# Cell and attention kernel: the last amplitude in the Sigmoid's scale, biases written by TensorE transposes, new instruction orders

## The chip, the cores and the metric

The kernel runs on one NeuronCore of a Trainium2 chip, as one launch. It is programmed engine by engine: TensorE (PE) multiplies and transposes, VectorE (DVE) and ScalarE (ACT) work elementwise, GpSimd (POOL) does small pieces and issues some DMAs, SyncE (SP) issues most DMAs. Each engine runs its own list of instructions in order, and semaphores are the only ties between the lists. The metric is the device time in microseconds, the median of several runs.

## The reference

A batch of 32 sequences of 64 tokens, 256 features, all f32. A sequence-dependent linear map feeds an attention with 16 heads of 16 features, in which five sines of each score are weighted and summed before a sigmoid. The result is normalised and added to x. Then comes an adapter chosen by language (down to 64, relu, up to 256, layer norm with its own gamma and beta), and a recurrence over the 32 sequences as time steps, with 64 tokens as its batch:

```python
for fi, freq in enumerate(FREQS):                     # 5 frequencies
    scores = scores + alpha[h, fi] * sin(TWO_PI * sim / freq + phi[h, fi])
w = sigmoid(scores); w = w / (sum(w, -1) + 1e-10)
out = layernorm(w @ v @ Wo.T + bo) * gamma + beta     # x = x + out
h = relu(hidden @ W1[lang] + b1[lang]);  x2 = hidden + h @ W2[lang] + b2[lang]
def step(c, xt):                                      # 32 steps
    ft = sigmoid(xt @ wf.T + c @ uf.T + bf); it = sigmoid(xt @ wi.T + c @ ui.T + bi)
    gt = tanh(xt @ wc.T + c @ uc.T + bc)
    return ft * c + it * gt, None
h = tanh(x @ wo.T + c_final @ uo.T + bo)              # x = x + h
```

## The kernel before

The 32 sequences form five groups of 4, 8, 8, 8 and 4 (`SIZES`). Per group: condition (one weight per sequence), turn to feature rows, queries, keys, values. The queries are spread into a block form by DMAs from SP (`spread_q(g, c)`; the first group is masked on the engines instead). Scores of a group are cut into as many *units* of 128x512 as it has sequences: for groups of eight a unit is one pair of heads (`pairs_of`), for the two groups of four it is two pairs, and everything with an amplitude or a phase is then two pieces of 256 columns.

For each unit `angle(n, f)` makes an integer phase for frequency f, either on ScalarE or on VectorE: ScalarE has the last `ON_ACT[n]` of the five frequencies, VectorE the others (105 of 160 on ScalarE). `wrap(n)` on VectorE masks all five at once, `sines(n)` on ScalarE takes the sines of all five, `add_sine(n, f)` on VectorE multiplies by the amplitude and adds up (f = 0 multiplies only), and `weights(n)` on ScalarE takes the sigmoid. `weighted(n)` on TensorE multiplies with the values, `divided` on VectorE divides by the sum.

The rest goes in eight parts of four sequences (q = 0 to 7): `turned`, an output row (`output_bias`: ScalarE writes the centred bias bo into PSUM, 128x512), `output_projection`, which adds on top of it, `squares`, `residual`, `turn_residual`, `adapter_down`, `hidden(q, 0)` (add b1), `hidden(q, 1)` (maximum with 0), `adapter_up`, `adapted`, `moments`, `normalise`, `turn_normed`, `modulated`, `shifted_language`. GpSimd computes the roots and issues three accumulating DMAs a part.

Cell step n needs a bias in its PSUM bank (`pg[n % 2]`, 128x384), written by ScalarE right after the tanh of step n-2, then `input_gates(n, 0 and 1)`, `state_gates(n)`, the tanh `gates(n)` on ScalarE, `cell_step(n, 0 and 1)` on VectorE, `state_turned(n)` on TensorE and `state_copy(n)` on VectorE. Sigmoids of the gates are taken as tanh of half the argument, so weights and biases are halved once (`halved`, `first_biases`). The output parts (`output_part`) are kept by ScalarE until the last state is known; the tail adds, takes a tanh and adds the residual.

The order on every engine is written out by hand, call by call, over all stages: neighbouring groups, parts and cell steps are interleaved. Products of the identity with itself, without use for the result, stand between the first stages on TensorE: 11 ahead of the first condition and 78 behind it. A product in f32 is two pieces in the trace, a transpose one. Four slots hold the angles of units in work (`SLOTS`). `LATE = 32` and `SUMMED = ()` switch two other variants off.

## Time and profile before

| what | us |
|---|---|
| median of 3 runs | 340.19 (338.52 to 341.05) |
| span of the profiled execution, first to last instruction | 337.2 |
| TensorE busy | 289.4 (86%) |
| VectorE busy | 285.0 (85%) |
| ScalarE busy | 270.5 (80%) |
| GpSimd busy | 49.4 (15%) |
| mean granted TensorE clock | 0.967 |

For the profiled execution only its span is known, and the durations all come from it. The rows of the last section but one are read so: PE is TensorE, PEld its weight loads, DVE VectorE, ACT ScalarE, SPq SyncE's own queue; L1667 is a line of the kernel; `sc<-ang,small,sc` is output and inputs by the program's names; `x19` is the number of pieces. Pieces on TensorE are pipelined: their durations overlap, and what one costs is better read from the distance of starts. A timeline merges neighbours of one kind, and a piece on VectorE or ScalarE can begin a little ahead of the end of its predecessor.

### The profile page before, as it was taken

How to read it: one execution, taken by the hardware profiler on the slowest of the kernel's cores; microseconds unless marked ns; L12 is line 12 of the kernel's file. 1: busy time of each engine (PE TensorE's matmuls, PEld its weight loads, DVE VectorE, ACT ScalarE, POOL GpSimd, SP SyncE). 2: the span in 40 equal slices, each digit the busy share in tenths (PEclk: the TensorE clock that was granted, in tenths of full speed). 3: DMA queues.
4: the chain of work that ended last, by engine and by line, in shares of the span. 5: the costliest groups of instructions: out<-in, count | busy, mean ns of one | idle time of the engine just before them, and what ended most of it. 6: DMA issues, size and time to landing. Idle time of an engine off the chain costs nothing.

```text
span 337.2 us, 7386 instructions
## 1 busy us (share of the span) xinstructions
PE 289.4 (86%) x2670; PEld 179.2 (53%) x2670; DVE 285.0 (85%) x617; ACT 270.5 (80%) x405; POOL 49.4 (15%) x58
## 2 busy tenths in 40 slices
PE   5979698396898899898999998899987998999873
PEld 5767278364455755454565544455653554433342
DVE  3189989969999999999999998999998999445256
ACT  1299999979999999999999999999999874323123
POOL 5000110012020004141000215302013212210000
PEclk9999999876999999999999999999997999999978
DMA  5688057563052485017723022700324150210006
GB/s 169 215 253 331 13 112 194 117 188 72 0 90 57 85 263 109 0 27 168 186 31 106 25 34 52 146 8 15 90 72 64 29 130 2 34 31 2 0 18 230
DMA packets 32230, 31.76 MB, mean 94 GB/s; under 512 B 10690, under 2 KB 24130, under 8 KB 32194
## 3 DMA queue, kind: packets, MB, share of 16 engines
q1 hardware_dynamic: 27266, 26.46, 28.7%
q0 software_dynamic: 4352, 4.20, 8.0%
q10 hardware_dynamic: 576, 0.64, 0.7%
q8 instruction: 21, 0.34, 0.4%
q14 instruction: 15, 0.12, 0.1%
HBM read 23.15 MB, written 2.10 MB: 75 GB/s over the span
## 4 chain that ended last, share of the span: by engine, by line
DVE 40%; ACT 21%; PE 17%; issue 10%; SPq 6%; DMA 2%; POOL 2%; DVEq 0%; ACTq 0%
DVE sc L1667 12%; ACT ang L1150 6%; DVE ang L1652 5%; PE pg L696 4%; ACT ang L1159 3%; DVE ang L1643 3%; SPq L343 3%; DVE fc L1806 2%; DVE sc L1665 2%; ACT gat L1205 2%; PE pf L606 2%; DVE vz L1633 1%; PE pr L670 1%; PE pf L526 1%; ACT sc L1141 1%
## 5 line engine op out<-in xcount | busy, mean ns | idle before, releaser
L1667 DVE SCALAR_TENSOR_TENSOR sc<-ang,small,sc 128x512 f32<-128x512 f32 (+1 forms) x160 | 97.8, 637 | 1.5
L1159 ACT ACTIVATE ang<-ang,qs 128x2560 f32<-128x2560 int32 x32 | 77.4, 2426 | 0.4 <-DVE ang L1652 0.2
L1150 ACT ACTIVATE ang<-sc,phase 128x512 int32<-128x512 f32 (+1 forms) x126 | 72.3, 641 | 0.7 <-DVE sc L1667 0.7
L687 PE MATMUL pg<-gate_w,zT 128*64 128x384 f32 x256 | 51.8, 504 | 1.1 <-ACT pg L1201 0.5
L696 PE MATMUL pg<-gate_u,cT 128*64 128x384 f32 x256 | 47.8, 494 | 3.0 <-DVE cT L1815 2.9
L1652 DVE TENSOR_SCALAR ang<-ang 128x2560 int32<-128x2560 int32 x32 | 47.4, 1483 | 1.9 <-ACT ang L1150 1.8
L1205 ACT ACTIVATE gat<-pg 128x384 f32<-128x384 f32 x32 | 15.6, 486 | 28.2 <-PE pg L696 28.1
L1643 DVE TENSOR_SCALAR ang<-sc,phase 128x256 int32<-128x256 f32 (+1 forms) x74 | 27.1, 406 | 4.7 <-ACT sc L1141 4.7
L696 PEld LDWEIGHTS pg<-gate_u,cT 128*64 128x64 f32 x256 | 16.6, 136 | 23.5 <-issue 14.8
L687 PEld LDWEIGHTS pg<-gate_w,zT 128*64 128x64 f32 x256 | 15.4, 137 | 18.6 <-issue 12.8
L1806 DVE SCALAR_TENSOR_TENSOR fc<-gat 128x256 f32<-128x256 f32 x32 | 13.4, 419 | 12.4 <-ACT gat L1205 12.2
L606 PE MATMUL pf<-qm,kT 64*64 64x128 f32 x512 | 18.8, 284 | 5.4 <-DMA qm<-qT 3.1
L624 PEld LDWEIGHTS pav<-vz,sc 128*64 128x64 f32 x512 | 18.1, 137 | 9.9 <-issue 5.6
L624 PE MATMUL pav<-vz,sc 128*64 128x34 f32 x512 | 19.7, 224 | 3.8 <-DVE atq L1687 2.9
L1141 ACT ACTIVATE sc<-pf 128x512 f32<-128x512 f32 x32 | 17.5, 592 | 4.1 <-PE pf L606 4.0
L1170 ACT ACTIVATE sc<-sc 128x512 f32<-128x512 f32 x32 | 19.2, 623 | 1.8 <-DVE sc L1667 1.7
L606 PEld LDWEIGHTS pf<-qm,kT 64*64 64x64 f32 x512 | 14.8, 138 | 10.4 <-issue 8.5
L526 PE MATMUL pf<-yT,wq 128*128 128x512 f32 (+1 forms) x40 | 16.1, 524 | 4.8 <-DVE yT L1619 3.4
L441 POOL TENSOR_SCALAR rs<-var 128x2 f32<-128x2 f32 x8 | 4.3, 536 | 104.3 <-ACT x L1186 104.3
L648 PE MATMUL pr<-wo,stage 128*128 128x256 f32 x64 | 17.8, 419 | 1.9 <-ACT pr L1179 1.8
L732 PE MATMUL pr<-wout,zT 128*128 128x256 f32 x64 | 17.9, 420 | 0.7 <-DVE zT L1796 0.7
L1665 DVE TENSOR_SCALAR sc<-ang,small 128x512 f32<-128x512 f32 (+1 forms) x40 | 16.4, 426 | 0.3 <-ACT ang L1159 0.2
(137 smaller groups left out, 482.9 us busy)
## 6 DMA issues: line engine op xcount, KB each, us to landing
wc<-in_cond SPq DMA_DIRECT2D x30, 257.0 KB, 3.4
w<-in_up SPq DMA_DIRECT2D x32, 128.2 KB, 2.6
wa<-in_down SPq DMA_DIRECT2D x32, 66.0 KB, 2.2
xt<-in_xt SPq DMA_DIRECT2D x8, 256.0 KB, 2.9
xt<-rows POOLq DMA_DIRECT2D x8, 256.0 KB, 4.2
w<-x POOLq DMA_DIRECT2D x8, 256.0 KB, 4.8
xg<-in_x SPq DMA_DIRECT2D x3, 512.0 KB, 5.7
qm<-qT SPq DMA_DIRECT2D x48, 32.0 KB, 2.2
```

What stands on the lines that cost most here:

```text
L606: mm = pe.matmul(pf[u * L:(u + 1) * L, r, k * P:(k + 1) * P], kT[r * L:(r + 1) * L, c, b * L:(b + 1) * L], qm[r * L:(r + 1) * L, b + (SPRE ...
L624: mm = pe.matmul(pav[r, col:col + 2 * HV], at[:, b * L:(b + 1) * L], vz[:, b, p, :, :].rearrange("p u d -> p (u d)"), start=True, stop=True)
L687: pe.matmul(pg[n % 2][u * L:(u + 1) * L, 0:GCOLS], zT[:, q % 2, kc, t * L:(t + 1) * L], gate_w[:, kc, u, :], start=False, stop=(kc == KC - ...
L696: mm = pe.matmul(pg[n % 2][u * L:(u + 1) * L, 0:GCOLS], cT[:, kc, :], gate_u[:, kc, u, :], start=False, stop=(kc == KC - 1), skip_group_ch ...
L1141: act.activation(sc[:, lo:lo + 2 * nb * L].rearrange("p (k b n) -> p b k n", k=2, n=L)[:, h * PB:(h + 1) * PB], pf[:, r, :].rearrange("p ( ...
L1150: op = act.activation(ang[:, n % SLOTS, f, r], unit(n)[:, r], ACT.Identity, scale=TURN / FREQS[f], bias=phase[:, p * NF + f:p * NF + f + 1])
L1159: act.activation(a.bitcast(F32), a, ACT.Sin, scale=2 * PI_LOW / TURN, bias=qs[:, 3:4]).then_inc(sine_ready, 1)
L1205: act.activation(gat[:, 0:GCOLS], pg[n % 2][:, 0:GCOLS], ACT.Tanh).then_inc(gate_ready, 1)
L1643: op = dve.tensor_scalar(ang[:, n % SLOTS, f, r], unit(n)[:, r], TURN / FREQS[f], phase[:, p * NF + f:p * NF + f + 1], ALU.mult, ALU.add)
L1652: dve.tensor_scalar(a, a, (1 << TURN_BITS) - 1, None, ALU.bitwise_and).then_inc(angle_ready, 1)
L1665: op = dve.tensor_scalar(unit(n)[:, r], sine, amp, None, ALU.mult)
L1667: op = dve.scalar_tensor_tensor(out=unit(n)[:, r], in0=sine, scalar=amp, in1=unit(n)[:, r], op0=ALU.mult, op1=ALU.add)
```

## The change

1. *Sum of the sines.* New constants `lead` (the amplitude of the last frequency, shifted by 2e-12 where it's below 1e-12) and `ratio` (amplitude over `lead`). `add_sine(n, 0)` adds the first sine, times its ratio, to the fifth sine; three further fused steps follow. The sigmoid gets `lead` as its scale, per partition and pair of heads, so that units of the first and last group need two activations.
2. *Gate bias.* For the steps in `BIAS_BY_PE` (14 of 32) three transposes of a broadcast bias put it into PSUM; ScalarE writes the other 18.
3. *Output row.* For parts 0 to 5 (`ROW_BY_PE`) four transposes put the row into PSUM. The row is turned once (`turn_output_row`) and kept by VectorE (`keep_output_row`). For parts 6 and 7 ScalarE writes it as before.
4. *Hidden layer.* Two instructions of 64 columns, each with add and maximum, in place of one add and one maximum of 128 columns.
5. *Shares.* `ON_ACT` sums to 93 instead of 105, so VectorE makes 12 more angles.
6. *Orders.* All engines' lists are rewritten. On SP the cell's constants are loaded ahead of the attention's, of x and of the weights of group 1, and the adapter loads of part 0 ahead of the first spread. The constants have one array more, the turned gate bias (128x384). On ScalarE the halving of biases and gate weights moves to the first group. On TensorE all 11 identity products ahead of the first condition go, and 63 instead of 78 remain behind it. On VectorE four additions of the tail come ahead of the first residual.

```diff
-ON_ACT = [2, 2, 3, 3, 3, 4, 3, 4, 3, 4, 3, 4, 3, 4, 3, 4, 3, 4, 3, 4, 3, 4, 3, 4, 3, 4, 3, 4, 3, 3, 3, 2]
+ON_ACT = [1, 2, 3, 1, 3, 4, 1, 4, 3, 4, 2, 4, 2, 3, 3, 4, 3, 4, 3, 3, 3, 3, 3, 3, 3, 4, 3, 4, 2, 3, 3, 2]
+LEAST = 1e-12
+BIAS_BY_PE = (0, 1, 2, 4, 6, 8, 10, 12, 14, 16, 17, 18, 24, 31)
+ROW_BY_PE = (0, 1, 2, 3, 4, 5)
...
@@ sync
+            load_rest_consts()
             load_attention_consts()
-
             load_x(1)
+            load_cond(1, 1)
+            load_cond(1, 3)
             load_cond(1, 0)
             load_cond(1, 2)
-            load_cond(1, 3)
-            load_cond(1, 1)
-            load_rest_consts()
-            spread_q(1, 0)
             load_rest(0, 0)
-            load_cond(2, 1)
             load_rest(0, 1)
             load_rest(0, 2)
+            load_rest(0, 3)
+            spread_q(1, 0)
+            load_cond(2, 2)
             load_x(2)
-            load_rest(0, 3)
+            load_cond(2, 1)
+            load_cond(2, 3)
             spread_q(1, 1)
...
@@ tensor
+            def turn_output_row():
+
+                pe.wait_ge(row_centred, 1)
+                for c in range(KC):
+                    mm = pe.matmul(pr[:, 1, c * P:(c + 1) * P], rows[:, 3, c * P:(c + 1) * P], eye[:, :],
+                                   start=(c == 0), stop=True, is_transpose=True, skip_group_check=True)
+                mm.then_inc(row_turned, 1)
+
+            def output_bias(q):
+
+                pe.wait_ge(at_ready, q + 1)
+                if q == 0:
+                    pe.wait_ge(row_kept, 1)
+                for j in range(2):
+                    for c in range(KC):
+                        pe.matmul(tiles(q)[:, j, c * P:(c + 1) * P], out_bT[:, c, :], eye[:, :],
+                                  start=(j == 0 and c == 0), stop=True, is_transpose=True, skip_group_check=True)
...
+            def gate_bias(n):
+
+                if n == 0:
+                    pe.wait_ge(bias_scaled, 1)
+                wait(pe, gate_ready, n - 1)
+                for c in range(GATES):
+                    pe.matmul(pg[n % 2][:, c * P:(c + 1) * P], gate_bT[:, c, :], eye[:, :],
+                              start=(c == 0), stop=True, is_transpose=True, skip_group_check=True)
...
             pe.wait_ge(eye_s, 16)
-            for k in range(2):
-                for c in range(GATES):
-                    pe.matmul(pg[k][:, c * P:(c + 1) * P], eye[:, :], eye[:, :], start=(c == 0), stop=True, skip_group_check=True)
-
             pe.wait_ge(eye_s, 16)
-            for _ in range(5):
-                pe.matmul(pct[:, :], eye[:, :], eye[:, :], start=True, stop=True)
             condition(0, 0)
...
@@ scalar
-                    act.activation(unit(n), unit(n), ACT.Sigmoid).then_inc(w_ready, 1)
+                if n == 0:
+                    act.wait_ge(amps_ready, 1)
+                act.wait_ge(score_ready, n + 1)
+                for p in pairs_of(n):
+                    r = pair_in(n, p)
+                    op = act.activation(unit(n)[:, r], unit(n)[:, r], ACT.Sigmoid, scale=lead[:, p:p + 1])
+                op.then_inc(w_ready, 1)
...
-                if n + 2 < B:
+                if n + 2 < B and n + 2 not in BIAS_BY_PE:
+                    act.wait_ge(bias_halved, 1)
                     act.wait_ge(gate_ready, n + 1)
-                    gate_bias(n + 2)
+                    act.activation(pg[n % 2][:, 0:GCOLS], gate_b[:, :], ACT.Copy).then_inc(bias_set, 1)
...
@@ vector
-                    amp = scal(C_ALPHA + p * NF + f)
-                    sine = ang[:, n % SLOTS, f, r].bitcast(F32)
-                    if f == 0:
-                        op = dve.tensor_scalar(unit(n)[:, r], sine, amp, None, ALU.mult)
-                    else:
-                        op = dve.scalar_tensor_tensor(out=unit(n)[:, r], in0=sine, scalar=amp, in1=unit(n)[:, r], op0=ALU.mult, op1=ALU.add)
-                op.then_inc(score_ready if f == NF - 1 else score_part, 1)
+                    other = ang[:, n % SLOTS, NF - 1, r].bitcast(F32) if f == 0 else unit(n)[:, r]
+                    op = dve.scalar_tensor_tensor(out=unit(n)[:, r], in0=ang[:, n % SLOTS, f, r].bitcast(F32),
+                                                  scalar=ratio[:, p * NF + f:p * NF + f + 1], in1=other, op0=ALU.mult, op1=ALU.add)
+                op.then_inc(score_ready if f == NF - 2 else score_part, 1)
...
+            def keep_output_row():
+
+                dve.wait_ge(row_turned, 1)
+                dve.tensor_copy(out_bT[:].rearrange("p c n -> p (c n)"), pr[:, 1, 0:KC * P]).then_inc(row_kept, 1)
...
+            def hidden(q):
+
+                dve.wait_ge(down_done, q + 1)
+                for j in range(2):
+                    op = dve.tensor_scalar(hT[:, q % 2, j, :], pr[:, q % 2, j * L:(j + 1) * L], w2[:, q % 2, j, D:D + 1], 0.0, ALU.add, ALU.max)
+                op.then_inc(h_ready, 1)
...
             tail_added(0)
             tail_added(1)
+            tail_added(2)
+            tail_added(3)
             tail_residual(0)
             tail_residual(1)
-            tail_added(2)
-            tail_added(3)
+            tail_added(4)
+            tail_added(5)
             tail_residual(2)
```

The orders of the last part on TensorE, before and after (steps 22 to 24, part 7):

```
before: state_gates(22) turned(7) turn_normed(6) state_turned(22) output_projection(7) input_gates(23, 1)
        state_gates(23) input_gates(24) input_gates(25, 0) state_turned(23) turn_residual(7) state_gates(24)
after:  state_gates(22) weighted(30) weighted(31) input_gates(23) state_turned(22) turned(7) state_gates(23)
        turn_normed(6) output_projection(7) state_turned(23) gate_bias(24) input_gates(24) state_gates(24)
```

## Rows read from the trace of the kernel before

**Rows 1.** stretches of the run; busy us and piece count per engine, granted TensorE clock, DMA share, GB/s
```profile
17.10:100.00 82.90, 66.62 (x622) 49.63 (x623) 74.40 (x144) 76.93 (x104) 8.15 (x8) 0.92 0.52 136
100.00:280.00 180.00, 163.60 (x1669) 96.05 (x1669) 175.46 (x380) 172.36 (x261) 31.56 (x33) 0.99 0.36 81
280.00:323.50 43.50, 38.06 (x251) 16.70 (x247) 21.98 (x64) 12.79 (x28) 5.29 (x8) 1.00 0.08 13
```

**Rows 2.** timeline of TensorE, 278 to 323 us: start, us, engine, line, operation
```profile
283.18 1.49 PE L696 MATMUL pg<-gate_u,cT 128*64 128x384 f32 x8
...
293.44 0.66 PE L534 MATMUL pr<-eye,x 128*128 128x128 f32 x4
294.02 1.51 PE L696 MATMUL pg<-gate_u,cT 128*64 128x384 f32 x8
...
309.17 1.51 PE L696 MATMUL pg<-gate_u,cT 128*64 128x384 f32 x8 [0.38 <-DVE cT L1815]
...
312.77 1.51 PE L696 MATMUL pg<-gate_u,cT 128*64 128x384 f32 x8 [0.38 <-DVE cT L1815]
```

**Rows 3.** VectorE by form, 100 to 280 us: group xcount, busy us, mean ns, idle before
```profile
L1643 DVE TENSOR_SCALAR ang<-sc,phase 128x512 int32<-128x512 f32 x24 | 11.0, 471 | 0.0
L1665 DVE TENSOR_SCALAR sc<-ang,small 128x512 f32<-128x512 f32 x19 | 9.1, 478 | 0.2 <-ACT ang L1159 0.2
```

**Rows 4.** VectorE by form, whole run
```profile
L1643 DVE TENSOR_SCALAR ang<-sc,phase 128x256 int32<-128x256 f32 x38 | 10.8, 344 | 2.5 <-ACT sc L1141 2.5
...
L1665 DVE TENSOR_SCALAR sc<-ang,small 128x256 f32<-128x256 f32 x16 | 4.9, 346 | 0.0
```

**Rows 5.** ScalarE by form, 100 to 280 us
```profile
L1150 ACT ACTIVATE ang<-sc,phase 128x512 int32<-128x512 f32 x56 | 36.8, 712 | 0.0
L1170 ACT ACTIVATE sc<-sc 128x512 f32<-128x512 f32 x26 | 15.4, 622 | 0.1
...
L1201 ACT ACTIVATE pg<-gate_b 128x384 f32<-128x384 f32 x22 | 10.9, 495 | 0.7
...
L1150 ACT ACTIVATE ang<-sc,phase 128x256 int32<-128x256 f32 x22 | 9.4, 496 | 0.0
...
L1179 ACT ACTIVATE pr<-rows 128x512 f32<-128x512 f32 x6 | 3.6, 595 | 0.2
```

**Rows 6.** ScalarE by form, whole run
```profile
L1112 ACT ACTIVATE qT<-pf,bqs,qs 128x512 f32<-128x512 f32 x6 | 4.6, 765 | 0.7 <-PE pf L526 0.7
...
L1119 ACT ACTIVATE kT<-pf,small 128x512 f32<-128x512 f32 x6 | 4.0, 672 | 0.0
...
L1231 ACT ACTIVATE gate_u<-gate_u 128x1024 f32<-128x1024 f32 x1 | 1.1, 1061 | 0.0
```

**Rows 7.** timeline of SP's DMA queue, 38 to 110 us
```profile
39.08 5.28 SPq L343 DMA_DIRECT2D qm<-qT  x8
...
55.99 6.34 SPq L343 DMA_DIRECT2D qm<-qT  x8
63.14 5.89 SPq L325 DMA_DIRECT2D wc<-in_cond  x6
```

**Rows 8.** timeline of TensorE, 56 to 100 us
```profile
64.08 1.10 PE L606 MATMUL pf<-qm,kT 64*64 64x128 f32 x32 [3.07 <-DMA qm<-qT]
```

**Rows 9.** timeline of VectorE, 36 to 72 us
```profile
59.10 2.45 DVE L1633 TENSOR_TENSOR vz<-pf,bv 64x1024 f32<-64x1024 f32 x2
```

**Rows 10.** timeline of TensorE, 0 to 18 us
```profile
2.78 2.93 PE L752 MATMUL pg<-eye 128*128 128x128 f32 x12 [2.78 <-DMA eye<-in_eye]
...
8.61 1.95 PE L548 MATMUL pf<-wc,xg 128*64 128x256 f32 x16 [0.91 <-DMA wc<-in_cond]
...
11.83 1.28 PE L763 MATMUL pct<-eye 128*128 128x128 f32 x10
```

**Rows 11.** timeline of VectorE, 322 to 337 us
```profile
326.64 1.29 DVE L1830 TENSOR_TENSOR go<-go,x 128x512 f32<-128x512 f32 x2
327.85 1.28 DVE L1824 TENSOR_TENSOR go<-go,hoc 128x512 f32<-128x512 f32 x2
329.23 1.29 DVE L1830 TENSOR_TENSOR go<-go,x 128x512 f32<-128x512 f32 x2
```

More of the change, by code:

```diff
@@ L273, in build @@
         banks = {4: pf[:, 0, :], 5: pf[:, 1, :], 6: pr[:, 0, :], 7: pr[:, 1, :]}
[L275 to L291 removed]
+        def slot_free(eng, n):
+            if n >= SLOTS:
+                eng.wait_ge(score_ready, n - SLOTS + 1)
         def shifted_wait(eng, q):
@@ L677, in turn_normed @@
                 turn(chunks(q), norm, 2, nt_done)
+            def gate_bias(n):
[5 more added lines that the diff above has]
+                              start=(c == 0), stop=True, is_transpose=True, skip_group_check=True)
             def input_gates(n, kc):
+                if kc == 0 and n not in BIAS_BY_PE:
+                    pe.wait_ge(bias_set, sum(k not in BIAS_BY_PE for k in range(n + 1)))
                 q, t = n // PB, n % PB
@@ L783, in _ @@
             condition(2, 1)
-            for _ in range(5):
-                pe.matmul(pct[:, :], eye[:, :], eye[:, :], start=True, stop=True)
+            warm(3)
             turn_tokens(1)
+            warm(5)
             queries(1, 0)
@@ L790, in _ @@
             keys(1, 1)
-            for _ in range(9):
-                pe.matmul(pct[:, :], eye[:, :], eye[:, :], start=True, stop=True)
+            warm(7)
             scores(2)
-            for _ in range(4):
-                pe.matmul(pct[:, :], eye[:, :], eye[:, :], start=True, stop=True)
-            scores(3)
             weighted(0)
             weighted(1)
-            for _ in range(5):
-                pe.matmul(pct[:, :], eye[:, :], eye[:, :], start=True, stop=True)
+            scores(3)
             weighted(2)
+            turn_output_row()
+            weighted(3)
+            warm(6)
+            turned(0)
             values(1, 0)
@@ L935, in _ @@
             state_turned(8)
-            input_gates(9, 1)
+            gate_bias(10)
+            input_gates(10, 0)
+            input_gates(10, 1)
+            scores(13)
             state_gates(9)
-            output_part(2, 1)
-            scores(13)
             turn_residual(3)
+            condition(7, 0)
+            turned(4)
+            adapter_down(3)
             state_turned(9)
-            turned(4)
-            input_gates(10, 0)
-            adapter_down(3)
-            input_gates(10, 1)
+            condition(7, 1)
@@ L954, in _ @@
+            keys(4, 0)
             turn_normed(3)
-            condition(7, 0)
-            condition(7, 1)
+            adapter_down(4)
+            queries(4, 1)
+            adapter_up(4)
+            input_gates(12, 0)
             state_turned(11)
-            input_gates(12, 0)
             input_gates(12, 1)
@@ L1318, in _ @@
             angle(9, 4)
+            tokens(3)
+            tokens(4)
+            sines(7, False)
             sines(8, False)
-            sines(9, False)
-            angle(10, 2)
             angle(10, 3)
             angle(10, 4)
+            queries(2, 0)
+            sines(9, False)
+            keys(2, 0)
+            queries(2, 1)
             angle(11, 1)
```

1124 lines of the change are left out of this document (515 added, 609 removed).

## The prediction

> **What bounds the kernel now.** I read the stretches first [rows 1]. From 17.1 to 100 us VectorE is busy 74.4 of 82.9 us and ScalarE 76.9; from 100 to 280 they are busy 175.5 and 172.4 of 180, and TensorE 163.6. From 280 to 323.5 TensorE alone is near full (38.1 of 43.5). So the long middle is held by two engines at once, with a third not far behind: an instruction taken from one of them is worth its own time only as far as the other two let it. Two other regimes stand around it. Before 100 us VectorE and ScalarE idle 8.5 and 6.0 us. After 280 us the cell recurrence sets the pace: two neighbouring state products start 3.60 us apart (309.17, 312.77) when nothing else is in the way, while the two steps from 283.18 to 294.02 took 10.84 us [rows 2]. Groups by form give the prices, in the middle and over the whole run [rows 3 to 6]; timelines give the rest.
>
> **The scores' sum (VectorE).** Per batch unit the first product, a plain multiplication, goes: the fifth sine is added unscaled in the first of four fused steps, and the common factor moves into the Sigmoid. In the middle 19 multiplications of 512 columns go, 9.1 us [rows 3]; units 28 to 31 have two of 256 columns each, and 4.9 us for the sixteen of eight units is 0.61 a unit, 2.4 us [rows 4]. Together 11.5 us. Before 100 us four units of the first group (2.4) and six of the second at 0.48 (2.9) give 5.3 us. That the first fused step now reads two sines instead of a sine and a score I take at nothing: same shape, same memory. With 10 ns more on each of the 40 first steps it'd be 0.4 us.
>
> **Angles moved from ScalarE to VectorE.** Twelve of 105: three in the first group, three in units 4 to 11, five in units 12 to 27, one in the last group. On VectorE one takes 0.471 us [rows 3], a pair of 256 columns 0.57 (10.8 us for 38 pieces [rows 4]); on ScalarE 0.712, or 0.85 a pair (9.4 us for 22 pieces [rows 5]). Middle: VectorE 5 x 0.471 + 0.57 = +3.0, ScalarE 5 x 0.712 + 0.85 = -4.4. Before 100 us: VectorE +3.1, ScalarE -4.7.
>
> **Sigmoid.** Its scale becomes a per-partition pointer. The nearest rows are two activations of 128x512 from PSUM, one with a pointer as bias (672 ns), one with pointers as scale and bias (765 ns): 93 ns for the pointer [rows 6]. For 24 units, 2.2 us. Units 0 to 3 and 28 to 31 need two pieces each instead of one: two angles of 256 columns take 0.85 us against 0.622 for the present Sigmoid [rows 5]; I take +0.3 a unit, between 0.2 and 0.4, so 1.2 before 100 us and 0.6 in the middle.
> The Trainium skill ("ScalarE: Activation LUTs", section "What ACT_TABLE_LOAD costs") says 93 ns for each such pointer, and the rows agree. By it this edit gives part of its gain back on the other full engine; the sum is the same by the page and by the rows.
>
> **Biases by TensorE.** In the middle ten of 22 gate biases leave ScalarE at 0.495 us, 5.0 us, and five of six output rows at 0.595, 3.0 us [rows 5]. The halving of the two gate matrices (1.06 us each [rows 6]) moves to before 100 us: 2.1. So ScalarE in the middle: 172.4 - 5.0 - 3.0 - 4.4 - 2.1 + 2.2 + 0.6 = 160.7. In their place TensorE gets 10 x 3 + 5 x 4 = 50 transposes of 128x128. Four such start within 0.58 us (293.44 to 294.02), 0.145 each, and last 0.66 with the pipe's end, 0.165 each [rows 2]: +7.3 to +8.3 us, from 163.6 to 171 or 172. The wait is not a new one: today the input product of step n waits for a bias that ScalarE writes after the tanh of step n-2, and the transposes wait for that same tanh. But the waiting instruction now stands in TensorE's own order, with scores, value products and state transposes queued behind it, and VectorE and ScalarE wait for those.
>
> **Hidden layer, kept row, constants.** The add and the maximum of the adapter become two pieces of half the columns, each with both operations, and one hand-over goes: -0.3 us in the middle, between -1 and 0. The copy of the turned output row is a piece of some 0.4 us before 100 us (an estimate from the 256-column pieces). The five new constants at the start lie in VectorE's wait for the first products.
>
> **The middle, summed.** VectorE 175.5 - 11.5 + 3.0 - 0.3 = 166.7, ScalarE 160.7, TensorE 171 to 172. VectorE with its present 4.5 us of idle time gives 171.2. TensorE's figure contains ends of the pipe that can overlap, so it's no hard floor, yet an engine this near to full will hold up the others. I take 173: a **gain of 7.0 us**. Bounds: 169 (half of VectorE's idle time gone as well, gain 11) and 180 (everything given back).
>
> **17 to 100 us.** VectorE -5.3 + 3.1 + 0.4 = -1.8; ScalarE -4.7 - 0.9 - 0.6 (two gate biases, one output row) + 0.4 (one more halving) + 2.1 + 1.2 = -2.5. I take **-1.8**. SP's order counts too. The spreads of the queries of group 1 start at 39.08 and 55.99, and the first lasts 5.28 [rows 7], so 11.6 us of other loads lie between. The nine adapter loads move ahead of the first spread, where SP stands idle; between the two there are now six condition weights and one of x. Six of the former take 5.89 us [rows 7]; with the x load some 6.5, so the second spread comes 5.1 us earlier. But the scores behind it start at 64.08 today [rows 8], and they also need the values, ready at 59.10 + 2.45 = 61.55 [rows 9]. That leaves **-2.0**, between 0 and -2.5. The constants' load moves ahead of x and the weights of group 1. I cost it at nothing, because VectorE has the first group's sines to add meanwhile, and at up to 4 us if those weights land late.
>
> **The start.** The products with the identity ahead of the first condition go. Twelve pieces of them took 2.93 us (0.24 each), ten equal ones later 1.28 (0.13) [rows 10]: TensorE began at the lower of its two levels (1.2 GHz) and rose after these pieces. Without them the first condition, 16 pieces in 1.95 us [rows 10], runs at the lower level: +1.9. The first turn and queries add some 0.4, the filler taken out between them gives 0.3 back. I take **+2.0**, between 0 and 4.
> The Trainium skill ("TensorE: Matmul & The Clock Gate", section "Part 4: PE-mode transpose") says that transposes don't count as busy for the clock in the way products do. No row here separates the two. By that rule the transposes wouldn't hold the clock up; that is rival 3.
>
> **The end.** The two slow steps cost 10.84 - 7.2 = 3.6 us more than two free ones, since the last part's output products stand between them. The new order puts those one step later, and three transposes (0.44) with them: **-1.0**, between 0 and -2. Behind the recurrence VectorE's additions and residuals go in pairs of 1.29 us; a pair of additions starts 1.21 after the residuals before it (326.64, 327.85), but residuals start 1.38 after additions (327.85, 329.23), which wait for a tanh [rows 11]. Four additions first save 0.17 twice: **-0.4**.
>
> **How the numbers follow.** -7.0 - 1.8 - 2.0 + 2.0 - 1.0 - 0.4 = -10.2 us. The profiled span is 337.2 us; the median of the runs, 340.2, lies 3.0 above it, and I keep that difference: span 327.0, time **330.0 us**.
>
> **Rivals.**
> (1) *TensorE becomes the bound of the middle.* Its 50 transposes stand in front of work that feeds the others, and the middle stays at 179. For it: the three engines need 167, 161 and 171 of 173 us, more than any stretch today. Against it: TensorE's figure counts pipe ends. Gain 1 instead of 7: 336.0 us; with the weights of group 1 late by up to 3 us, 339.
> (2) *All of the saving comes through.* ScalarE has 6 us more slack than VectorE, so idle time shrinks, and the start costs nothing: -11 - 1.8 - 2.5 - 2 - 0.5 = -17.8, 322.4 at the extreme, 325 as its middle. Against it: TensorE's load.
> (3) *The clock falls, and the time ends above today's.* From 17.1 to 100 us the granted clock is 0.92 on average [rows 1], that is 13 us at the lower level. Of the 78 filler products behind the start 63 remain, and 50 transposes stand in the middle. At the lower level TensorE, being full there, loses half a microsecond for each. It decides from 20 us of it in the middle (10.2 / 0.5); with 25 us, -10.2 + 12.5 = +2.3, 342.5 us. Against it: the middle has 0.99 today without a filler, so its own products hold the clock.
> (4) *The change doesn't do what it says*: ScalarE holds the middle, and a shorter sum on VectorE brings nothing. ScalarE would have to need 172; the rows give 161. Time 338 to 340.
>
> **Chances.** The forecast and its surroundings (326.5 to 334) 0.50, (2) 0.15, (1) 0.22, (3) 0.10, (4) 0.03. Some 1% is what a measurement of this kernel can tell from no change. Faster by over 1% (below 336.8): 0.50 + 0.15 + 0.13 of (1) = 0.78; within 1%: 0.12; slower: 0.10. The range 322 to 339 leaves out (3) and the far ends of (2), (1) and (4).
>
> **What the profile would show.** No plain multiplications of sines; 160 fused steps of today's length; Sigmoids of 512 columns near 715 ns; 18 gate biases and two output rows left on ScalarE; TensorE above 95% busy in its middle; the first condition at twice its length; the last unit's Sigmoid, and with it the end of the middle, some 8 to 9 us earlier. The prediction is wrong if VectorE's idle time in the middle grows by more than 6 us, if the clock there is below 0.9, or if group 1 starts more than 4 us later.

## The result, and the profile after

The changed kernel takes **322.5 us** (median of 4 runs, 320.6 to 324.2) against 339.4 of the kernel before beside it (338.5 to 341.1): a ratio of 0.949, 95% interval 0.944 to 0.954. The forecast was 330.0 with a range of 322 to 339. The sign was right and the time lies in the range, but at its lower edge: 16.9 us came where 10.2 were forecast. The profiled run took 323.4 us, 1.8 above its span. A run more than 1.5% above the fastest of its kernel is left out of median and ratio, which matters below for a_spold alone (five of ten).

The page of the changed kernel, first part and slices (each digit is the busy share of a fortieth of the span):

```profile
span 321.6 us, 7374 instructions
...
PE 285.4 (89%) x2686; PEld 177.5 (55%) x2686; DVE 274.6 (85%) x598; ACT 257.3 (80%) x378; POOL 51.6 (16%) x58
...
DVE  3049996999999999999999998999999998554265
ACT  1069998999999999999999999899999894422132
...
PEclk9999997998999999999999999999999999999997
```

VectorE's busy time fell from 285.0 to 274.6 us and ScalarE's from 270.5 to 257.3. The prediction's terms, added up, give VectorE 10.6 us less. So the work is as forecast, and the surprise is elsewhere: the span shrank by 15.6 us, more than either engine's work. To find the place, cut both runs at the same three events: the copy of the first scores (ScalarE), the last unit's Sigmoid and the last tanh of the gates. These are the stretches of the kernel before, with a cut at 100 us (columns as in [rows 1]):

```profile
17.11:100.00 82.89, 66.62 (x622) 49.63 (x623) 74.40 (x144) 76.93 (x104) 8.15 (x8) 0.92 0.52 136
100.00:282.01 182.01, 165.61 (x1693) 97.01 (x1691) 177.47 (x385) 173.11 (x262) 31.56 (x33) 0.99 0.36 80
282.01:321.53 39.52, 35.72 (x232) 15.60 (x228) 18.97 (x55) 11.55 (x26) 5.29 (x8) 1.00 0.09 15
```

and these the same of the changed kernel:

```profile
20.43:100.00 79.57, 69.54 (x646) 50.38 (x646) 75.59 (x146) 75.85 (x101) 10.63 (x8) 0.96 0.50 133
100.00:268.49 168.49, 163.18 (x1703) 99.02 (x1704) 166.01 (x361) 161.79 (x240) 32.53 (x34) 1.00 0.37 83
268.49:305.90 37.41, 35.51 (x245) 16.17 (x239) 18.71 (x54) 10.81 (x24) 4.05 (x7) 1.00 0.05 8
```

- Before the first scores: 17.11 to 20.43, **+3.3 us**.
- From the first scores to the last Sigmoid: 264.90 to 248.06, **-16.8 us**. VectorE's part of that: 251.9 busy becomes 241.6 (-10.3), and 13.0 idle becomes 6.5 (-6.6). The idle time shrank on both sides of the cut: 8.5 to 4.0 before 100 us, 4.5 to 2.5 behind it.
- The recurrence: 39.52 to 37.41, **-2.1 us**. These 2.1 aren't made in the recurrence itself, as the part on the recurrence below shows.
- From the last tanh to the end of the span: 15.7 in both.

The groups that the change touches, by form, whole run of the changed kernel (count | busy us, mean ns | idle just before them and its releaser), VectorE's first:

```profile
L1626 DVE SCALAR_TENSOR_TENSOR sc<-ang,ratio,sc 128x512 f32<-128x512 f32 x72 | 52.6, 743 | 0.2
L1615 DVE TENSOR_SCALAR ang<-ang 128x2560 int32<-128x2560 int32 x32 | 47.5, 1501 | 0.0
...
L1626 DVE SCALAR_TENSOR_TENSOR sc<-ang,ratio 128x512 f32<-128x512 f32 x24 | 17.8, 742 | 0.0
```

```profile
L1149 ACT ACTIVATE sc<-sc,lead 128x512 f32<-128x512 f32 x24 | 16.4, 714 | 0.3 <-DVE sc L1626 0.2
...
L1183 ACT ACTIVATE pg<-gate_b 128x384 f32<-128x384 f32 x18 | 8.9, 495 | 1.6
...
L1149 ACT ACTIVATE sc<-sc,lead 128x256 f32<-128x256 f32 x16 | 7.0, 500 | 2.0 <-DVE sc L1626 2.0
```

The plain multiplications of [rows 3, 4] are gone. A first step that reads two sines lasts 742 ns, one that reads a sine and a sum 743. The Sigmoid with its pointer lasts 714 ns (forecast near 715), and 18 gate biases and two output rows are left on ScalarE.

TensorE in the middle of the changed kernel, in stretches of 20 us:

```profile
120.00:140.00 20.00, 19.38 (x165) 11.18 (x162) 19.91 (x37) 19.97 (x28) 5.92 (x7) 1.00 0.44 114
140.00:160.00 20.00, 19.78 (x213) 10.90 (x211) 19.97 (x44) 19.47 (x27) 4.65 (x4) 1.00 0.51 104
160.00:180.00 20.00, 19.94 (x238) 13.00 (x235) 19.68 (x39) 19.75 (x27) 0.00 (x0) 1.00 0.45 109
```

All three engines read 97 to 100% here, and the granted clock is 1.00, its full level (2.4 GHz), with the transposes in and without a product of the identity. The case that the prediction thought unlikely, three full engines at once without one holding up another, is what the trace shows: VectorE idles 0.4 of these 60 us.

The clock before 100 us changed too: it reads 0.92 from 17 to 100 us before and 0.96 in the changed kernel, some 13 and 6 us at the lower level (1.2 GHz). A stretch where it is low in the kernel before:

```profile
67.00:76.00 9.00, 9.00 (x72) 6.15 (x72) 5.88 (x9) 6.60 (x12) 1.18 (x2) 0.71 0.65 190
```

TensorE is full there at a clock of 0.71, and VectorE idles 3.1 of its 8.5 us. In the changed kernel the same 9 us have a clock of 0.81, TensorE is busy for 6.6 us and VectorE for 8.9. So part of the idle time that vanished before 100 us may be the clock's. No run changes the clock alone, so its share isn't shown.

### The profile page after: what moved, and what is told of

Its sections match the earlier page's. It is cut to its first block, busy times and chain, and to the rows that moved or that the text cites. A ratio compares the mean times of both kernels' runs of the same rounds, so it can differ in the third digit from the quotient of the medians.

```text
span 321.6 us, 7374 instructions
## 1 busy us (share of the span) xinstructions
PE 285.4 (89%) x2686; PEld 177.5 (55%) x2686; DVE 274.6 (85%) x598; ACT 257.3 (80%) x378; POOL 51.6 (16%) x58
## 4 chain that ended last, share of the span: by engine, by line
DVE 39%; PE 32%; ACT 14%; issue 8%; DMA 3%; POOL 2%; SPq 1%; DVEq 0%; ACTq 0%; POOLq 0%
DVE sc L1626 12%; PE pg L694 7%; DVE ang L1615 5%; PE pg L685 5%; DVE ang L1606 5%; ACT ang L1130 4%; PE pf L491 3%; PE pav L589 3%; ACT ang L1139 3%; PE pf L571 2%; PE pf L547 2%; DVE fc L1761 2%; ACT sc L1121 2%; DMA w<-x 1%; DVE vz L1596 1%
## 5 line engine op out<-in xcount | busy, mean ns | idle before, releaser
L1626 DVE SCALAR_TENSOR_TENSOR sc<-ang,ratio,sc 128x512 f32<-128x512 f32 (+1 forms) x120 | 73.0, 637 | 0.4
L1130 ACT ACTIVATE ang<-sc,phase 128x512 int32<-128x512 f32 (+1 forms) x110 | 64.5, 650 | 0.0
L685 PE MATMUL pg<-gate_w,zT 128*64 128x384 f32 x256 | 50.8, 499 | 0.6 <-DVE zT L1751 0.4
L1606 DVE TENSOR_SCALAR ang<-sc,phase 128x256 int32<-128x256 f32 (+1 forms) x90 | 32.4, 412 | 2.6 <-ACT sc L1121 2.5
L1179 ACT ACTIVATE gat<-pg 128x384 f32<-128x384 f32 x32 | 15.6, 487 | 22.7 <-PE pg L694 22.3
L694 PEld LDWEIGHTS pg<-gate_u,cT 128*64 128x64 f32 x256 | 16.4, 136 | 22.1 <-issue 15.0
L513 PE MATMUL pf<-wc,xg 128*64 128x256 f32 x128 | 17.1, 416 | 9.5 <-DMA wc<-in_cond 8.8
L1149 ACT ACTIVATE sc<-sc,lead 128x512 f32<-128x512 f32 (+1 forms) x40 | 23.4, 628 | 2.3 <-DVE sc L1626 2.2
L1626 DVE SCALAR_TENSOR_TENSOR sc<-ang,ratio 128x512 f32<-128x512 f32 (+1 forms) x40 | 24.8, 637 | 0.0
L491 PE MATMUL pf<-yT,wq 128*128 128x512 f32 (+1 forms) x40 | 17.0, 550 | 1.9 <-DVE yT L1582 1.4
L729 PE MATMUL pct<-eye 128*128 128x128 f32 x126 | 18.2, 291 | 0.0
```

The costliest lines, as they stand in the source:

```text
L491: mm = pe.matmul(dst[:, 0:n], w[:, kc, oc * P:(oc + 1) * P], src[:, kc, 0:n], start=(kc == 0), stop=(kc == KC - 1))
L685: pe.matmul(pg[n % 2][u * L:(u + 1) * L, 0:GCOLS], zT[:, q % 2, kc, t * L:(t + 1) * L], gate_w[:, kc, u, :], start=False, stop=(kc == KC - ...
L694: mm = pe.matmul(pg[n % 2][u * L:(u + 1) * L, 0:GCOLS], cT[:, kc, :], gate_u[:, kc, u, :], start=False, stop=(kc == KC - 1), skip_group_ch ...
L1130: op = act.activation(ang[:, n % SLOTS, f, r], unit(n)[:, r], ACT.Identity, scale=TURN / FREQS[f], bias=phase[:, p * NF + f:p * NF + f + 1])
L1149: op = act.activation(unit(n)[:, r], unit(n)[:, r], ACT.Sigmoid, scale=lead[:, p:p + 1])
L1606: op = dve.tensor_scalar(ang[:, n % SLOTS, f, r], unit(n)[:, r], TURN / FREQS[f], phase[:, p * NF + f:p * NF + f + 1], ALU.mult, ALU.add)
```

## The experiments

The theory on record, **A**: the time follows the work taken off VectorE and ScalarE, and the new orders add a little. The rival, **B**: the orders carry the gain. Twelve kernels were run, in three groups of four, with the kernel before at 340.4 to 340.7 us in each, so times can be compared across them. The changed kernel itself ran beside one at 339.4; by its ratio it would be at 323.3 among them, so differences to its 322.5 are uncertain by about 1 us. Each kernel has one trace; what a stretch of it lasted is one execution's. "Operations" below are the folded amplitude, the transposed biases and rows, and the adapter's step; "shares" is the number of angles per unit that ScalarE makes; a "list" is an engine's order of work.

### The operations without the orders

b_sum is the kernel before with the folded amplitude alone. The core of the edit; the ratios and the Sigmoid's scale go with it:

```diff
-                    if f == 0:
-                        op = dve.tensor_scalar(unit(n)[:, r], sine, amp, None, ALU.mult)
...
+                    other = ang[:, n % SLOTS, NF - 1, r].bitcast(F32) if f == 0 else unit(n)[:, r]
```

> The kernel before, with the folded amplitude alone (four fused steps, Sigmoid with a pointer scale); its orders and shares stay. Theory A, two full engines share the middle: VectorE loses 16 us of pieces, ScalarE gets 5.6 us more and is full, so little comes through: 335 to 339 us. Rival, VectorE alone holds the middle: 10 us or more come through, 329 us or less.

Measured: 341.6 us, ratio 1.004 (1.001 to 1.007). VectorE has 11.3 us less to do (273.7), ScalarE 3.6 more (274.1), and the kernel is no faster: theory A's 335 to 339 is missed as well as the rival's 329. The middle, in stretches of 50 us:

```profile
100.00:150.00 50.00, 44.42 (x532) 28.74 (x531) 46.87 (x86) 49.78 (x72) 6.66 (x8) 1.00 0.41 96
150.00:200.00 50.00, 45.23 (x507) 26.82 (x507) 45.96 (x91) 49.72 (x73) 6.22 (x7) 1.00 0.44 96
```

ScalarE is full (99.5%), VectorE at 92 to 94%. With the old shares ScalarE is the fullest engine of the middle, and its Sigmoids have just become longer.

b_ops takes all of the new operations, with the old lists, shares and identity products (the new steps put at the places of the old):

```diff
+            gate_bias(0)
             input_gates(0, 0)
...
+            output_bias(1)
             output_projection(1, 0)
```

> All new operations (folded amplitude, 14 gate biases and 6 output rows by transposes, the merged hidden step), but the orders, the shares of the angles and the identity products of the kernel before. Theory A, the work taken from both full engines is the gain: 328 to 331 us, with VectorE's idle time before 100 us still near 8 us. Rival, the new orders and shares carry the gain: 334 us or more. Rival, TensorE is the bound with its 68 transposes: 336 us or more, with VectorE's idle time in the middle grown.

Measured: 340.2 us, ratio 0.998 (0.995 to 1.001). Now both are relieved (VectorE 285.0 to 274.4, ScalarE 270.5 to 265.3), and nothing comes of it:

```profile
100.00:150.00 50.00, 47.24 (x556) 30.72 (x556) 47.24 (x88) 49.03 (x72) 6.64 (x9) 1.00 0.39 93
150.00:200.00 50.00, 47.52 (x522) 28.31 (x520) 46.77 (x92) 48.75 (x69) 5.59 (x7) 1.00 0.44 95
200.00:250.00 50.00, 46.91 (x457) 28.91 (x455) 47.01 (x108) 45.44 (x64) 9.16 (x9) 1.00 0.31 65
```

No engine is full behind 200 us, and VectorE idles 3 us in each 50. What it waits for from 100 to 250 us (total us, times, longest) is spread over many hand-overs:

```profile
DVE fc L1776 <- ACT gat L1182: 2.1, 2, 1.4
DVE rden L1654 <- PE pav L590: 1.4, 3, 0.6
DVE sc L1641 <- ACT ang L1142: 1.2, 2, 0.8
...
DVE ang L1630 <- ACT ang L1133: 0.5, 1, 0.5
```

The last line is the wrap, which needs all five angles of its unit. In the whole run VectorE waits 3.7 us before its wraps, against 1.9 in the kernel before and 0.0 in the changed one, but only 0.5 of that falls between 100 and 250 us. Cut at the same events, b_ops is 2.7 us shorter from the first scores to the last Sigmoid (262.2, with VectorE's work 11.3 us less and its idle time 8.7 us more). It gives this back at the start (the copy of the first scores comes at 18.76, 1.7 later: its 11 products ahead of the condition all go to one bank, and the condition's 16 pieces take 3.68 us) and in the recurrence (1.6). So the operations do a little in the old lists, and the sum hides it.

Theory A, as I had put it, falls here: 328 to 331 was expected. The expectation's third case, TensorE as the bound with its 68 transposes, isn't excluded by b_ops alone: 336 us or more with VectorE's idle time grown is what came, TensorE is 94 to 95% busy, and ScalarE waits 2.4 us for its state products from 100 to 250 us. But b_sum, which has no transpose of a bias, is no faster either, so the transposes aren't needed to explain it. The transposes are also cheaper than forecast: TensorE is busy 5.8 us longer in b_ops than in b_sum, 0.085 for each of the 68 (0.12 by a_bias_act below), against the 0.145 to 0.165 of the prediction.

### The orders without the operations

a_old_ops_sh is the reverse: the changed kernel's five lists, with the old operations and the old shares. It still makes the new constants and keeps the turned row (VectorE is busy 287.5 us, 2.5 more than in the kernel before), and it has six products with the identity ahead of the first condition.

```diff
-ON_ACT = [1, 2, 3, 1, 3, 4, 1, 4, 3, 4, 2, ...]
+ON_ACT = [2, 2, 3, 3, 3, 4, 3, 4, 3, 4, 3, ...]
...
+            output_row(0)
...
             add_sine(0, 3)
+            add_sine(0, 4)
```

> The changed kernel's five order lists with every old operation put back (plain first product and five steps of a sum, one Sigmoid over the unit, all gate biases and output rows written by ScalarE, the adapter's bias and maximum in two steps) and the old shares of angles. If the orders alone carry the gain, the removed 10.4 us of VectorE and 13.2 us of ScalarE being slack: 322 to 326. If the new orders made VectorE the engine that limits, so that each microsecond of its work is one of the time: 322.5 + 10.4 and the start's 1.6 back, 331 to 334. If neither operations nor orders are worth anything without the other: 337 or more.

Measured: 347.1 us, ratio 1.019 (1.013 to 1.025), **slower than the kernel before**. B falls as well, in its simple form. The orders alone lose 6.5 us, the operations alone gain 0.2, and everything together gains 16.9.

### SyncE's and GpSimd's lists

a_loads is the changed kernel with the nine adapter loads of the first part back between the two spreads of group 1:

```diff
-            load_rest(0, 0)
...
-            load_rest(0, 3)
             spread_q(1, 0)
+            load_rest(0, 0)
...
+            load_rest(0, 3)
             load_cond(2, 2)
```

> The changed kernel with the nine adapter loads of part 0 put back behind the first spread of group 1, as in the kernel before. If these loads made the idle time between 60 and 100 us, the second spread comes some 10 us later, VectorE idles 4 to 6 us more before 100 us and the time is 326 to 328 us. Rival, the idle time vanished for other reasons: 322 to 323 us.

Measured: 327.1 us, ratio 0.962 (0.957 to 0.967), 4.6 above the changed kernel. The second spread in it, and then both spreads in the changed kernel (start, us, operation):

```profile
63.36 5.21 SPq L309 DMA_DIRECT2D qm<-qT  x8
```

```profile
41.76 6.25 SPq L309 DMA_DIRECT2D qm<-qT  x8
...
55.44 5.40 SPq L309 DMA_DIRECT2D qm<-qT  x8
```

The second spread starts 7.9 us later, the scores behind it 5.3 later (64.97 to 70.31), and in a_loads they have waited for it:

```profile
70.31 1.98 PE L571 MATMUL pf<-qm,kT 64*64 64x128 f32 x32 [6.57 <-DMA qm<-qT]
```

The changed kernel shows no such wait there. VectorE is busy 3.9 us less from 20 to 100 us (71.7 instead of 75.6).

a_spold puts both old lists of SyncE and GpSimd into the changed kernel, a_spnew adds the new ones to b_ops, b_sp to the kernel before.

```diff
-            load_rest_consts()
             load_attention_consts()
             load_x(1)
...
+            load_rest_consts()
+            spread_q(1, 0)
```

> The changed kernel with SyncE's and GpSimd's lists of before. Putting nine loads back behind the first spread alone cost 4.6. If that is all that SyncE's order is worth: 326 to 329. If the new compute orders stand on the new loads throughout: 333 or more. If the loads matter only there and elsewhere the old order is as good: 326.

Measured: 337.1 us (333.8 to 338.5; with the five left out 339.1, up to 343.4), ratio 0.986 (0.981 to 0.992): most of the gain is lost with two lists in which next to no computation stands. The waits of a_spold from 18 to 45 us (total us, times, longest):

```profile
ACT gate_bT L1199 <- DMA uout<-in_uout: 8.6, 1, 8.6
...
PE pf L500 <- ACT xg L1084: 8.2, 1, 8.2
DVE ang L1616 <- ACT ang L1131: 7.5, 1, 7.5
```

ScalarE's new list has the halving of biases and gate weights near its start, and it waits there for the last of the constants. With the constants loaded late, it stands 8.6 us with the copy of x and the angles of unit 2 queued behind it, and TensorE and VectorE stand with it. In the changed kernel the same stretch has no such wait. If that and the adapter loads (4.6) simply add up, they are 13.2 of the 14.6 us lost; the constants' place wasn't run by itself. The rest of SyncE's list is in it too: from 120 to 160 us VectorE idles 3.9 us in a_spold, and part of what it waits for hangs on condition weights that land late. Its clock from 20 to 100 us reads 0.91, the changed kernel's 0.96.

> All new operations, the old orders of TensorE, VectorE and ScalarE and the old shares, but the new lists of SyncE and GpSimd. If SyncE's order is worth its 4.6 us by itself: 335 to 337 (340.2 less 4). If it is worth something only where the compute lists ask for the earlier data: 339 to 342.

Measured: 336.4 us, ratio 0.987 (0.983 to 0.991): -3.8 to b_ops.

> The kernel before with the new lists of SyncE and GpSimd alone. With the new operations these lists gave 3.8 us in the old compute orders (340.2 to 336.4). If that gain is independent of the operations: 336 to 337. If it needed their saving: 339 to 342.

Measured: 338.3 us, ratio 0.996 (0.992 to 0.9995): -2.3. The number agrees with the 2.0 of the prediction (by the interval it may be 0.2 to 2.9), the way there only in part: the second spread starts at 53.22 instead of 55.99, 2.8 us earlier where 5.1 were forecast, and the scores behind it at 63.09, 1.0 earlier. The same loads are worth 2.3 us there, 3.8 with the new operations, and 14.6 (322.5 to 337.1) where the compute lists rely on them.

### One operation undone in the changed kernel

a_nofold has the old sum and Sigmoid in the new lists and shares (the plain product stands ahead of the first fused step).

```diff
             add_sine(0, 0)
+            add_sine(0, 1)
...
-                    op = act.activation(unit(n)[:, r], unit(n)[:, r], ACT.Sigmoid, scale=lead[:, p:p + 1])
+                act.activation(unit(n), unit(n), ACT.Sigmoid).then_inc(w_ready, 1)
```

> The changed kernel with the sum of sines as before (plain first product and four fused steps on VectorE, one Sigmoid over the unit on ScalarE); biases, rows, adapter, orders and shares stay new. VectorE has some 11 us more, ScalarE some 3.5 less. With everything undone and the old shares the time was 347.1, 24.6 above the changed kernel. If VectorE's work is what the new orders are built round: 333 to 338, over half of the 24.6. If the gate biases on ScalarE matter as much: 327 to 330.

Measured: 338.1 us, ratio 0.992 (0.989 to 0.994). VectorE is busy 291.4 us, 16.8 more than in the changed kernel (the expectation's 11 was the middle's part alone of the 16.8 in the prediction), and the time is 15.6 longer: 0.93 us for each us of VectorE. ScalarE's Sigmoids by form:

```profile
L1145 ACT ACTIVATE sc<-sc 128x512 f32<-128x512 f32 x32 | 19.5, 626 | 8.3 <-DVE sc L1625 8.3
```

ScalarE waits 8.3 us for VectorE's sums, 2.3 in the changed kernel. The fold that brought nothing in the old lists (b_sum) is worth nearly its full work in the new. One caution holds for this run and the next two: the new lists were made for the new operations and shares, so an operation put back costs its own time and also stands where no place was left for it. The two can't be told apart here.

a_bias_act gives all gate biases back to ScalarE, the first two right behind the halving, and has TensorE write six products with the identity into the gates' banks ahead of the first condition:

```diff
-BIAS_BY_PE = (0, 1, 2, 4, 6, 8, 10, 12, 14, 16, 17, 18, 24, 31)
+BIAS_BY_PE = ()
...
+            for k in range(2):
+                for c in range(GATES):
+                    pe.matmul(pg[k][:, c * P:(c + 1) * P], eye[:, :], eye[:, :], start=(c == 0), stop=True, skip_group_check=True)
```

> The changed kernel with all 32 gate biases written by ScalarE, none by transposes: 14 more ScalarE writes of about 0.49 us (6.9 us, most of them in the middle), 42 transposes less on TensorE (7.3 us in the profile). If ScalarE has no slack in the new orders: 327 to 331. If TensorE is the engine that limits, as its 97 to 99% between 120 and 200 us suggests: 318 to 321. If neither: 322 to 324.

Measured: 325.7 us, ratio 0.955 (0.952 to 0.957), +3.2. ScalarE has 5.8 us more (263.1), TensorE 2.1 less (42 transposes gone, 5.0 us or 0.12 each, and six products of together 2.9 us come). The time is what ScalarE's 5.8 us cost less what TensorE's relief gave, and only the sum is measured: 0.55 us for each us of ScalarE. So a bias costs more on ScalarE than on TensorE. That TensorE's 97 to 100% held up nobody isn't shown by it.

a_shares gives ScalarE back its twelve angles:

```diff
-ON_ACT = [1, 2, 3, 1, 3, 4, 1, 4, 3, 4, 2, 4, ...]
+ON_ACT = [2, 2, 3, 3, 3, 4, 3, 4, 3, 4, 3, 4, ...]
```

> The changed kernel with the old shares of angles: 12 angles of a frequency go from VectorE to ScalarE, at the place of ScalarE's other angles of the unit. VectorE's busy time falls by 5 to 8 us, ScalarE's rises by about 8 to 265. If VectorE's work alone sets the time: 315 to 319. If the two are balanced by the new shares, so that ScalarE's extra work shows: 325 to 330. If both have slack: 322 to 323.

Measured: 327.2 us, ratio 0.961 (0.955 to 0.966), +4.7, though VectorE has 3.6 us less to do; ScalarE has 6.7 more (264.0). So in the new lists an added us costs on either engine, as with two balanced engines, with the caution above.

### The start

a_warm puts 11 products with the identity ahead of the first condition, as many as the kernel before has there:

```diff
+            warm(11)
             condition(0, 0)
```

> The changed kernel with the 11 identity products put back ahead of the first condition. Theory: the first scores' copy comes 3.3 us earlier (17.1 instead of 20.4) and the whole follows: 319 to 320 us. Rival, the weights of group 1 or something else is late anyway and takes it back: 322 us, no difference.

Measured: 320.6 us (319.7 to 324.0), ratio 0.945 (0.938 to 0.952). This interval overlaps that of the changed kernel (0.944 to 0.954), so the 1.9 us aren't clear of the noise. a_best has 15, and 3 behind the condition:

```diff
+            warm(15)
             condition(0, 0)
             condition(0, 1)
+            warm(3)
             turn_tokens(0)
```

> The changed kernel with 15 identity products ahead of the first condition and 3 behind it (the first condition was still 3.46 us long behind 11, with 1.20 us idle ahead of it, against 1.95 us in the kernel before). If the idle time ahead of it is what halves the clock: condition 1.9 to 2.0 us, first scores' copy ends 3 us earlier than in the changed kernel, 318 to 319.5. If not: 320 to 322.5 as with 11.

Measured: 319.7 us (318.7 to 320.4), ratio 0.937 (0.935 to 0.940), **the lowest of all**, and clear of the changed kernel though not of a_warm. TensorE at the start of the changed kernel, of a_warm, of a_best, and of a_loads, which begins on TensorE as the changed kernel does:

```profile
8.84 3.68 PE L513 MATMUL pf<-wc,xg 128*64 128x256 f32 x16 [8.84 <-DMA wc<-in_cond]
13.30 1.11 PE L499 MATMUL pf<-eye,xg 128*128 128x128 f32 x4 [0.78 <-ACT xg L1083]
...
15.30 2.01 PE L491 MATMUL pf<-yT,wq 128*128 128x256 f32 x4
...
19.26 1.10 PE L571 MATMUL pf<-qm,kT 64*64 64x128 f32 x32 [0.42 <-ACT kT L1099]
```

```profile
2.63 5.03 PE L729 MATMUL pct<-eye 128*128 128x128 f32 x22 [2.63 <-DMA eye<-in_eye]
8.87 3.46 PE L513 MATMUL pf<-wc,xg 128*64 128x256 f32 x16 [1.20 <-DMA wc<-in_cond]
...
17.73 1.10 PE L571 MATMUL pf<-qm,kT 64*64 64x128 f32 x32 [0.42 <-ACT kT L1100]
```

```profile
2.66 6.33 PE L729 MATMUL pct<-eye 128*128 128x128 f32 x30 [2.66 <-DMA eye<-in_eye]
9.03 1.95 PE L513 MATMUL pf<-wc,xg 128*64 128x256 f32 x16
...
16.38 1.10 PE L571 MATMUL pf<-qm,kT 64*64 64x128 f32 x32 [0.42 <-ACT kT L1101]
```

```profile
9.01 3.61 PE L513 MATMUL pf<-wc,xg 128*64 128x256 f32 x16 [9.01 <-DMA wc<-in_cond]
13.40 0.66 PE L499 MATMUL pf<-eye,xg 128*128 128x128 f32 x4 [0.77 <-ACT xg L1083]
...
18.02 1.10 PE L571 MATMUL pf<-qm,kT 64*64 64x128 f32 x32 [0.42 <-ACT kT L1099]
```

The condition's 16 pieces last 3.68 us with nothing ahead of them, 3.46 with 11 products and then 1.20 us of idle time, and 1.95 with 15 products up to its start. The scores start at 19.26, 17.73 and 16.38, and the times go the same way: 322.5, 320.6, 319.7. But with nothing ahead of the condition the scores start anywhere from 17.69 (a_spold) over 18.02 (a_loads) and 18.10 (a_nofold) to 19.68 (a_shares), so a_warm's 17.73 isn't shown to come from its products. Only a_best's 16.38 lies apart. Which of its 15 and 3 products does it wasn't run separately.

### The table

| Operations | shares | SyncE, GpSimd lists | compute lists | us |
|---|---|---|---|---|
| old | old | old | old | 340.6 |
| new | old | old | old | 340.2 |
| old | old | new | old | 338.3 |
| new | old | new | old | 336.4 |
| new | new | old | new | 337.1 |
| old | old | new | new | 347.1 |
| new | old | new | new | 327.2 |
| new | new | new | new | 322.5 |

## Why the prediction was right, and where it was wrong

**Work.** Every count and duration came as forecast: VectorE -10.4 us (forecast -10.6), Sigmoids of 714 ns, the first step's two sines at no cost, the condition at nearly twice its length, TensorE above 95%.

**The middle.** This is the term that was mis-sized. The step that failed is: "an engine this near to full will hold up the others. I take 173". I had VectorE's idle time of the middle grow from 4.5 to 6.3 us; it fell to 2.5 behind 100 us. TensorE's 171 to 172 never came either: it is busy 163.2 us in the changed kernel's 168.5. The middle has 1703 of its pieces where the kernel before has 1693, not 50 more, since the new lists put other work of TensorE elsewhere, and a transpose added 0.085 to 0.12 us of busy time, not 0.145 to 0.165. From the first scores to the last Sigmoid the terms gave -10.8 (7.0, 1.8 and 2.0), and 16.8 came; of the missing 6.0, all is idle time of VectorE. a_bias_act shows that the transposes were the cheaper choice: with 42 of them turned back into writes of ScalarE the time rose.

**Why idle time fell.** The prediction weighed the operations for themselves and the compute lists at nothing. The runs show that neither counts alone: the operations in the old lists give 0.2 us, the lists without them cost 6.5. In the old lists and shares a relieved VectorE waits instead, for ScalarE and TensorE at many hand-overs, none of which stands out. In the new ones a us put back on VectorE costs 0.93 and the twelve moved angles 4.7. Before 100 us, where 4.5 of the 6.6 us of idle time went, the loads' order and the clock changed as well; a_loads gives the adapter loads 3.9 us of VectorE's time there. Rival (4), that a shorter sum brings nothing because ScalarE holds the middle, got 0.03; for the kernel before it comes near (b_sum), and what made it wrong for this change are the shares and orders. The time that came is that of rival (2), all of the saving (0.15): it names the shrinking idle time. Its start at no cost didn't come.

**SyncE's order.** Forecast -2.0; in the kernel before it is -2.3 (b_sp), in part by luck, since the scores there come 1.0 earlier and not 2.0. In the changed kernel itself the second spread starts at 55.44, 0.6 us earlier than before and not 5.1, because the first one starts 2.7 later. With the new lists the adapter loads alone are worth 4.6, because the scores behind the second spread then wait for nothing else. The constants' earlier load I cost at nothing to +4 us; it is in fact what ScalarE's early halving needs, and the wait without it is 8.6 us. I had moved the halving's 2.1 us from one stretch to another and had not asked what it waits for.

**The start.** Forecast +2.0, measured +3.3. The condition's 1.7 is in it, and in this execution the turn and queries were long too: 1.11 and 2.01 us, against 0.66 and 1.04 in the kernel before. In a_loads, a_nofold and a_spold, which begin the same way, they took 0.66 and 1.13, and the scores started 1.8 to 2.2 us later than in the kernel before: the forecast's 2.0. a_best takes 2.8 us off the time. That TensorE was at its lower level there is read from durations alone, here and in the prediction: the clock column reads 1.00 from 8 to 16 us in both kernels.

**The recurrence.** Forecast -1.0, measured -2.1, but in another place. The last state products before, and the same steps (22, 24, 27 and 31) in the changed kernel:

```profile
305.46 1.51 PE L696 MATMUL pg<-gate_u,cT 128*64 128x384 f32 x8
...
319.97 1.51 PE L696 MATMUL pg<-gate_u,cT 128*64 128x384 f32 x8 [0.39 <-DVE cT L1815]
```

```profile
267.64 1.51 PE L694 MATMUL pg<-gate_u,cT 128*64 128x384 f32 x8
...
277.64 1.46 PE L694 MATMUL pg<-gate_u,cT 128*64 128x384 f32 x8
...
289.94 1.51 PE L694 MATMUL pg<-gate_u,cT 128*64 128x384 f32 x8 [0.38 <-DVE cT L1770]
...
304.34 1.51 PE L694 MATMUL pg<-gate_u,cT 128*64 128x384 f32 x8 [0.38 <-DVE cT L1770]
```

The slow pair of [rows 2], steps 22 to 24, went from 10.84 to 10.00 us. But steps 24 to 27 went from 11.44 to 12.30. From step 22 to the last it is 36.79 before and 36.70 after: putting the last part's products a step later moved the delay and removed nothing. The stretch is shorter because step 22 now starts 0.85 us before the last Sigmoid, where it started 1.17 behind it. The forecast's sign is right here by luck.

**The end.** Forecast -0.4, measured 0. Four additions do run back to back, but ScalarE then waits 1.17 us for the next pair:

```profile
309.62 2.50 DVE L1779 TENSOR_TENSOR go<-go,hoc 128x512 f32<-128x512 f32 x4
...
313.24 1.29 DVE L1779 TENSOR_TENSOR go<-go,hoc 128x512 f32<-128x512 f32 x2
313.96 1.23 ACT L1193 ACTIVATE go<-go 128x512 f32<-128x512 f32 x2 [1.17 <-DVE go L1779]
```

**The clock.** Rival (3) didn't come: the middle has 1.00 with 50 transposes more. Before 100 us the clock rose, from 0.92 to 0.96, which no term of the prediction has. It isn't small change: the two runs of the changed kernel with a mean clock of 0.989 took 320.6 and 321.6 us, the two with 0.982 and 0.983 took 324.2 and 323.4. The Trainium skill ("TensorE: Matmul & The Clock Gate", section "Part 4: PE-mode transpose") lets transposes count less for the clock than products; with products standing between them all through the middle no run here shows a difference.

**What stays open.** Of the 13.9 us from a_spnew to the changed kernel the shares are 4.7 (a_shares). The other 9.2 are the lists of TensorE, VectorE and ScalarE and the identity products between them; these three lists depend on one another, and one old beside two new wasn't run. Which hand-over gives the most isn't settled, nor what the clock before 100 us gives.

## What to carry to other kernels

Where several engines with fixed orders are each over 95% busy, an instruction's duration is no price by itself: the same forty multiplications on VectorE (16.4 us) were worth nothing in one set of orders and shares and 15.6 us in another. Price the operations, the shares and the orders together, and when an operation is made cheaper, make the orders anew before calling it useless. When a set-up step moves forward in a list, ask what it waits for: that load must move first, here 8.6 us. And a busy share of 97 to 100% on a third engine isn't yet a bound; look whether anyone waits for it. When a stretch has shrunk between two events, follow the steps inside it one by one: the recurrence here is 2.1 us shorter between its cuts and no faster.

## What the runs showed of the hardware

Eleven products with the identity ahead of the first condition left its 16 pieces at 1.95 or 1.96 us in three traces (the kernel before, with 0.91 us of idle time behind the products [rows 10], b_sum with 1.84, b_sp with 1.58). They left them at 3.33 to 3.68 us in three others (b_ops with 0.71, a_warm with 1.20, a_spnew with 2.01). With none they took 3.26 to 3.68 us. So neither the number of products nor the idle time behind them decides alone. In the first three the first six products go to the gates' banks, in the other three all go to one, and no run shows that this is the reason. Fifteen products up to the condition's start left it at 1.95 (a_best, one trace). From 8 to 12 us the clock column reads 1.00 in all of these but a_spnew (0.66), also where the pieces took twice as long.

All three compute engines were 97 to 100% busy together for 60 us: VectorE's fused steps lasted 743 ns in both kernels beside ScalarE and TensorE at those loads.
